# Reordering companion jobs, one output stage a pair earlier: a two-layer gated cross-attention kernel on one core

## The chip, the cores and the metric

One core of a Trainium2 chip runs the whole program in one launch. The metric is device time in microseconds, the median of several executions. Every time called "of the profile" comes from one further execution that was recorded instruction by instruction.

## The reference, cut to what matters

```
x = x + tanh(g_xattn[0]) * attn0(layernorm(x), ctx, ctx, mask)   # 16 heads of 32, no output projection
x = x + tanh(g_ffn[0])   * ffn0(layernorm(x))                    # 512 -> 2048 -> 2048 -> 2048 -> 512, SwiGLU, exact GELU
x = x + tanh(g_xattn[1]) * (attn1(layernorm(x), ctx, ctx) @ Wo.T + bo)
x = x + tanh(g_ffn[1])   * ffn1(layernorm(x))                    # 8-bit activations, ternary weights
```

`x` is 8 batches of 100 tokens of 512 numbers, `ctx` is 8 batches of 722 keys of 512. Queries, keys and values are float32, and the products of attentions and of the first feed-forward stage are made from a high and a low part of each operand (three products for each in the attentions), which is why most work comes in two halves: ScalarE (ACT) writes the high part, VectorE (DVE) or GpSimd (POOL) the low part.

## The kernel before, in words

The program has four stages in order of time: attention 0 (about 0 to 500 us), feed-forward 0 (500 to 1013 us), attention 1 (to about 1500 us) and feed-forward 1 (to the end). `L` is 0 or 1 for the attention.

An attention runs over `NP` = 64 pairs of heads, 8 pairs for each batch; `i` is the pair, `p` is `i % 8`. Each engine has its instructions in an order written out by hand, and engines wait for each other by semaphores alone. In pair `i` TensorE (PE) makes `scores(i + 1)`, `turn(i)` (the transposes of the exponentials), the companions of the pair, and `weigh(i - 1)` (the product with the values). DVE makes two `peak`s (the maxima of the scores of pair i + 1), `low_weighed(i - 2)` (takes the result of `weigh` out of PSUM), `low_turned(i)`, and the low part of each companion. ACT makes `high_weighed(i - 2)`, `high_turned(i)`, two `weights` (the exponentials of pair i + 1) and the high part of each companion. `scores(i + 1)` waits for the exponentials of pair i, since it overwrites their bank.

Companions are the projections of later batches, spread over the pairs by the table `BESIDE`: `("v", db, kt)` is a tile of 128 keys of V, `("k", db, g, half)` is half of the keys for K group `g` (four heads). The last, short tile of V of a batch is the tail job (`tail_job`, `high_tail`, `low_tail`, at the pairs of `tail_at`), packed with rows of the next batch. K halves are written to a staging tile `kst` (one for all groups, high and low), stored to HBM by `store_k`, and loaded in another layout by `load_k` into `KS`. `high_job` of a K half waits until the store of the group before has left its half of `kst`. The DMA orders are all given by SyncE (SP), in the order of its own loop.

The results of companions, of `weigh`, and of `project`, `turn_sums`, `turn_out` and `turn_normal` all go to two PSUM banks in turn. The list `RINGS` gives the turn order, and `ring_free(item)` makes PE wait until the item two places before has been taken out of its bank. For an item `("pv", i)` that is DVE's `low_weighed(i)`, for `("out", n)` DVE's `add_projected(n)`, and for `("xn", b)` ACT's `keep_normal`.

In attention 0 the finished batch b goes through `turn_out`, `add_out`, `stats_out`, `batch_root` (POOL), `normal_out` and `turn_normal` while later batches are worked on. In its last eight pairs `weigh` is made of 18 small products (`summed`), and there are no companions besides the one of pair 56.

At the end of attention 1 the 800 rows are cut into 7 output tiles. For tile n ACT and POOL write a high and a low part of the attention's result (`high_out`, `low_out`), PE multiplies by Wo (`project`, 12 products), SP has loaded the residual rows (`load_rows`), POOL has added the bias to them (`add_bo`), and DVE adds the product (`add_projected`) and takes mean and variance (`stats_projected`). POOL makes inverse roots (`tile_roots`), and `normal`, `scale_rows` and `quantize` lead to `turn_rows`, with which feed-forward 1 (`gate_and_up` first) begins. `OUT_AT` says in which pair each tile is projected.

## Time and profile before

| | us |
|---|---|
| median of 3 runs | 1588.3 |
| lowest and highest of them | 1586.6, 1588.71 |
| the profiled execution, whole | 1586.92 |
| its span (first to last instruction) | 1584.5 |
| PE busy in the span | 1565.0 |
| DVE busy | 1026.0 |
| ACT busy | 971.0 |
| POOL busy | 423.9 |

2.4 us of the profiled execution lie outside its span. Busy time of PE is a modelled figure: one matmul's end overlaps the next one's start, so a gap is a little longer than the idle time shown in brackets.

### The profile page before, as it was taken

To read this page: it belongs to the slowest core of one execution; us is meant where nothing else is said; L and a number is where in the kernel's file an instruction comes from. 1 tells how busy PE (TensorE), PEld (TensorE's weight loads), DVE (VectorE), ACT (ScalarE), POOL (GpSimd) and SP (SyncE) were. 2 spreads that over 40 slices of the span, in tenths; PEclk is the share of its full clock that TensorE was granted. 3 is DMA by queue.
4 is the path that set the end of the run, shared out by engine and by line. 5 is a ranking of instruction groups with operands and counts; after the bars stand their busy time and mean duration, and the time that the engine had idled before them with its cause. 6 is when DMAs were issued, how large, how long until landed. Compare 5 with 4: busy or idle time off the path is not lost.

```text
span 1584.5 us, 25762 instructions
## 1 busy us (share of the span) xinstructions
PE 1565.0 (99%) x9322; PEld 1427.5 (90%) x9322; DVE 1026.0 (65%) x1815; ACT 971.0 (61%) x2014; POOL 423.9 (27%) x569
## 2 busy tenths in 40 slices
PE   9999999999999999999999999999999999999999
PEld 7899899889888999999999998889999989988765
DVE  6577887787785563223544325647777777778987
ACT  5576777677665455444544435446677767666676
POOL 4121221222134222222222222311211121123751
PEclk9999999999999999999999999999999999999999
DMA  7766767677582325554365652576676677667500
GB/s 244 189 169 168 196 176 195 162 203 182 137 218 83 99 89 188 176 195 161 99 228 195 222 162 90 176 187 172 161 195 174 167 189 179 172 147 209 197 13 30
DMA packets 149974, 261.28 MB, mean 165 GB/s; under 512 B 41137, under 2 KB 94001, under 8 KB 149710
## 3 DMA queue, kind: packets, MB, share of 16 engines
q1 hardware_dynamic: 149505, 259.24, 58.3%
q8 instruction: 85, 1.39, 0.4%
q14 instruction: 52, 0.42, 0.1%
q10 hardware_dynamic: 332, 0.23, 0.0%
HBM read 191.01 MB, written 58.57 MB: 158 GB/s over the span
## 4 chain that ended last, share of the span: by engine, by line
PE 87%; DVE 6%; ACT 3%; DMA 2%; issue 1%; POOL 1%; SPq 0%; DVEq 0%; ACTq 0%
PE ps L1218 33%; PE ps L852 14%; PE ps L856 13%; PE ps L952 7%; PE ps L930 6%; PE ps L1152 2%; PE ps L1018 2%; PE ps L914 2%; PE ps L919 1%; DVE nmax L1367 1%; PE ps L1169 1%; PE ps L872 1%; ACT P L1909 1%; DVE PT L1373 1%; DMA kd<-ksl 1%
## 5 line engine op out<-in xcount | busy, mean ns | idle before, releaser
L1218 PE MATMUL ps<-ah_f,wh_f 128*128 128x400 f32 (+1 forms) x1296 | 442.9, 343 | 0.0
L1218 PE MATMUL ps<-al_f,wh_f 128*128 128x400 f32 (+1 forms) x1296 | 442.2, 342 | 0.0
L2272 POOL TENSOR_TENSOR cxl<-raw,cxh 128x384 fp32r<-128x384 f32 (+1 forms) x112 | 105.7, 965 | 562.7 <-ACT cxh L1851 562.7
L1773 DVE TENSOR_TENSOR wl_f<-raw_f,wh_f 128x1024 fp32r<-128x1024 f32 x85 | 103.7, 1223 | 231.9 <-POOL wh_f L2262 231.8
L1218 PEld LDWEIGHTS ps<-al_f,wh_f 128*128 128x128 f32 x1296 | 243.8, 188 | 0.0
L1218 PEld LDWEIGHTS ps<-ah_f,wh_f 128*128 128x128 f32 x1296 | 243.5, 188 | 0.1
L1367 DVE TENSOR_REDUCE nmax<-ps 100x1 f32<-100x722 f32 x256 | 220.6, 902 | 35.0 <-PE ps L918 31.4
L1909 ACT ACTIVATE P<-ps,nmax 100x722 f32<-100x722 f32 x256 | 219.9, 862 | 30.1 <-DVE nmax L1367 30.1
L1921 ACT ACTIVATE PT<-ps 128x400 fp32r<-128x400 f32 x384 | 165.9, 505 | 70.4 <-PE ps L930 69.2
L2190 ACT ACTIVATE raw_f<-wl_f 128x1024 f32<-128x1024 f32 x88 | 93.4, 1061 | 173.6 <-DVE wl_f L1773 173.0
L1373 DVE TENSOR_TENSOR PT<-ps,PT 128x400 fp32r<-128x400 f32 x384 | 196.3, 566 | 4.3 <-ACT PT L1921 1.1
L2262 POOL CAST wh_f<-raw_f 128x1024 fp32r<-128x1024 f32 x85 | 92.4, 1087 | 335.1 <-PE ps L1218 326.0
L852 PE MATMUL ps<-cxh,wkh 128*128 128x338 f32 (+1 forms) x512 | 173.3, 339 | 0.9 <-DVE cxl L1337 0.6
L852 PE MATMUL ps<-cxh,wkl 128*128 128x338 f32 (+1 forms) x512 | 167.8, 328 | 0.0
L852 PE MATMUL ps<-cxl,wkh 128*128 128x338 f32 (+1 forms) x512 | 167.0, 326 | 0.0
L952 PE MATMUL ps<-PT,V 128*128 128x400 f32 x720 | 152.2, 346 | 2.9 <-DVE V L1359 1.7
L930 PE MATMUL ps<-ident,P 100*128 100x100 f32 (+1 forms) x1536 | 153.1, 249 | 1.2 <-DVE PT L1373 1.2
L930 PEld LDWEIGHTS ps<-ident,P 100*128 100x128 f32 (+1 forms) x1536 | 143.1, 137 | 12.0 <-ACT P L1909 1.5
L952 PEld LDWEIGHTS ps<-PT,V 128*128 128x128 f32 x720 | 129.3, 188 | 10.2 <-DVE V L1359 6.5
L856 PE MATMUL ps<-wvh,cxh 128*128 128x512 f32 x320 | 131.5, 411 | 0.8 <-DVE V L1347 0.8
L1347 DVE SCALAR_TENSOR_TENSOR ksl<-ps,cols,ksh 128x384 fp32r<-128x384 f32 (+1 forms) x120 | 70.8, 590 | 94.9 <-ACT ksh L1862 94.9
L856 PE MATMUL ps<-wvh,cxl 128*128 128x512 f32 x320 | 126.1, 394 | 0.0
(226 smaller groups left out, 2665.2 us busy)
## 6 DMA issues: line engine op xcount, KB each, us to landing
KS<-kd SPq DMA_DIRECT2D x192, 361.0 KB
raw_f<-in_h SPq DMA_DIRECT2D x64, 512.0 KB, 3.9
raw_f<-in_gud SPq DMA_DIRECT2D x48, 512.0 KB, 4.3
raw<-in_ctx SPq DMA_DIRECT2D x64, 192.0 KB, 3.6
raw_f<-in_w SPq DMA_DIRECT2D x24, 512.0 KB, 3.9
kd<-ksh SPq DMA_DIRECT2D x60, 192.0 KB, 2.2
kd<-ksl SPq DMA_DIRECT2D x60, 192.0 KB, 2.5
raw<-in_ctx SPq DMA_DIRECT2D x64, 169.0 KB, 4.5
```

Of the source, the lines that this page charges most:

```text
L852: ins = e.matmul(o, m.wk[x][:, k, 128 * j[2]:128 * j[2] + 128], m.cx[y][:, k, off:off + n], start=(k == 0 and c == 0), stop=(k == 3 and c ...
L856: ins = e.matmul(o, m.cx[y][:, k, 128 * kt:128 * kt + KM[kt]], m.wv[x][:, k, :], start=(k == 0 and c == 0), stop=(k == 3 and c == 2))
L930: ins = e.transpose(ps[0:KM[kt], bank, o:o + S], m.P[0:S, (2 * i + h) % 3, 128 * kt:128 * kt + KM[kt]], ident[0:S, 0:S])
L952: ins = e.matmul(o, m.V[b % 2][0:r, kt, g, 128 * pr:128 * pr + 128], m.PT[0:r, i % 2, :, kt, :], start=(kt == 0), stop=(kt == KT - 1))
L1218: return e.matmul(o, p, q, start=start, stop=stop)
L1367: e.tensor_reduce(m.nmax[0:S, c:c + 1], scores_of(n), AX.X, ALU.max, negate=True).then_inc(v_max, 1)
L1373: e.tensor_tensor(lo, ps[:, bank, 0:400].rearrange("p (k n) -> p k n", k=2), raw32(hi), ALU.subtract).then_inc(v_t, 1)
L1773: e.tensor_tensor(wl[:, z, :], raw[:, r, :], raw32(wh[:, z, :]), ALU.subtract).then_inc(v_ul, 1)
L1909: e.activation(m.P[0:S, n % 3, :], scores_of(n), ACT.Exp, bias=m.nmax[0:S, c:c + 1], accum_out=m.rs[0:S, r:r + 1]).then_inc(a_exp, 1)
L1921: e.activation(m.PT[:, i % 2, 0, 2 * x:2 * x + 2, :], ps[:, bank, 0:400].rearrange("p (k n) -> p k n", k=2), ACT.Copy).then_inc(a_t, 1)
L2190: e.activation(raw[:, r, :], raw32(wl[:, z, :]), ACT.Abs, accum_out=low[:, z, 0:1]).then_inc(a_raw, 1)
L2272: e.tensor_tensor(m.cx[1][:, k, off:off + n], m.raw[:, k, off:off + n], raw32(m.cx[0][:, k, off:off + n]), ALU.subtract).then_inc(g_cx, 1)
```

## The change

1. `BESIDE`: in pair `p` = 4 K group 2's first half comes ahead of group 0's second half.
2. `tail_at`: the tail job of batch 0 goes from pair 1 to the end of pair 0, on PE, ACT and DVE. In the other pairs with a tail ACT takes it out between the two exponentials and not behind both.
3. Attention 0: the normalized rows of batch 5 (`normal_out`, `turn_normal`, `keep_normal`) go from pairs 56 and 57 to pairs 57 and 58, and DVE does `low_weighed(55)` ahead of both peaks of pair 57 instead of between them.
4. Attention 1: tile n is projected in pair 57 + n, not 58 + n. Its residual rows, bias, addition, statistics, roots, scaling and quantizing go with it by a pair each (the statistics of tiles 4 and 5 stand at pairs 61 and 63), and in pair 56 the first two tiles' rows are loaded ahead of that pair's `store_k`. `turn_rows(0)` stands behind `weigh(62)` and not ahead of it.

The amount of work is the same. The core of the diff (helpers of one line and the repetition of 2 in the ring lists are left out):

```
-          (("k", 1, 0, 1), ("k", 1, 2, 0)),
+          (("k", 1, 2, 0), ("k", 1, 0, 1)),
...
-    return i // 8 if i < NP and i % 8 == 1 and i // 8 % 4 < 3 else None
+    return i // 8 if i < NP and (i == 0 or i > 8 and i % 8 == 1) and i // 8 % 4 < 3 else None
...
+    if i == NP - 6:
+        return KEPT - 1
-    return i // 8 - 2 if i % 8 == 1 and 16 < i < NP else None
+    return i // 8 - 2 if i % 8 == 1 and 16 < i < NP - 8 else None
...
-OUT_AT = {58 + i: i for i in range(TILES - 1)}
+OUT_AT = {57 + i: i for i in range(TILES - 1)}
-STATS_AFTER = (59, 60, 61)
+STATS_AFTER = (58, 59, 60)
-OUT_FIRST = (60, 62)
+OUT_FIRST = (59, 61)
...
# SyncE
+                    if L and i == 56:
+                        w.wait_ge(p_pv, NP + 56)
+                        for n in range(2):
+                            load_rows(n)
                     for j in beside(i):
                         if j[0] == "k":
                             store_k(L, m, *j[1:])
...
                     if L and i == 57:
-                        w.wait_ge(p_pv, NP + 56)
-                        for n in range(4):
+                        for n in range(2, 4):
                             load_rows(n)
...
# TensorE
-                    if tail_at(i) is not None:
+                    if i and tail_at(i) is not None:
                         tail_job(tail_at(i))
                     for j in beside(i):
                         job(j)
+                    if i == 0:
+                        tail_job(0)
                     if L and i in OUT_AT:
                         project(OUT_AT[i])
+                    if i:
+                        weigh(i - 1)
                     if L and i == NP - 1:
                         turn_rows(0)
-                    if i:
-                        weigh(i - 1)
...
# VectorE
-                    early = scaled_at(i) is not None or L == 0 and i < NP - 7 and (
-                        out_at(i) is not None or turned_at(i) is not None)
-                    between = L == 0 and i == NP - 7
+                    early = scaled_at(i) is not None or L == 0 and (i == NP - 7 or i < NP - 7 and (
+                        out_at(i) is not None or turned_at(i) is not None))
...
+                    if L and i == 58:
+                        add_projected(0)
...
                     if i < NP:
                         low_turned(i)
-                    if L and i == 61:
+                    if L and i == 58:
+                        stats_projected(0)
+                    if L and i == 60:
                         scale_rows(0)
                     if L and i == 63:
                         inverse(B - 1)
                         scale_rows(1)
+                        stats_projected(5)
...
-                    if L == 0 and i == NP - 8:
+                    if L == 0 and i == NP - 7:
                         normal_out(i // 8 - 2)
...
+                    if i == 0:
+                        low_tail(0)
...
-                    if L and i in OUT_AT:
+                    if L and i in OUT_AT and i > 57:
                         add_projected(OUT_AT[i])
-                    if L and i in OUT_AT and i not in STATS_AFTER:
-                        stats_projected(OUT_AT[i])
+                    if L and i == 61:
+                        stats_projected(4)
...
# ScalarE
                     if i + 1 < NP:
                         weights(2 * i + 2)
+                    if i and tail_at(i) is not None:
+                        high_tail(tail_at(i))
                     if len(beside(i)) < 2 and i + 1 < NP:
                         weights(2 * i + 3)
-                    if L == 0 and i == NP - 7:
+                    if L == 0 and i == NP - 6:
                         keep_normal(turned_at(i))
...
                     for j in beside(i)[1:]:
                         high_job(j)
+                    if i == 0:
+                        high_tail(0)
...
# GpSimd
+                    if L and i == 58:
+                        tile_roots(0)
                     if L and i == 59:
-                        tile_roots(0)
-                    if L and i == 60:
                         normal(0)
-                    if L and i == 62:
+                    if L and i == 61:
                         quantize(0)
                     if L and i + 1 in OUT_AT:
                         low_out(OUT_AT[i + 1])
-                    if L and i == 60:
+                    if L and i == 59:
                         tile_roots(1)
                     if L and i == 57:
                         add_bo(0)
-                    if L and (57 <= i < 61 or i == 62):
-                        add_bo(min(i - 56, 5))
-                    if L and i == 63:
+                        add_bo(1)
+                    if L and 58 <= i < 62:
+                        add_bo(i - 56)
+                    if L and i == 62:
                         tile_roots(2)
```

## Rows read from the trace of the kernel before

**Rows 1.** The page, part 1: busy time and share of each engine.

```profile
PE 1565.0 (99%) x9322; PEld 1427.5 (90%) x9322; DVE 1026.0 (65%) x1815; ACT 971.0 (61%) x2014; POOL 423.9 (27%) x569
```

**Rows 2.** Windows: length, then busy us of PE, PEld, DVE, ACT, POOL.

```profile
1457.00:1500.00 43.00, 41.27 (x238) 32.83 (x237) 40.58 (x95) 28.42 (x66) 32.65 (x51) 1.00 0.74 238
```

**Rows 3.** Waits of PE over the span: us in total, times, longest.

```profile
PE ps L914 <- ACT P L1909: 2.2, 4, 0.7
PE ps L917 <- ACT P L1909: 2.0, 6, 0.4
PE ps L952 <- DVE V L1359: 1.7, 6, 0.4
...
PE ps L952 <- DVE ksl L1347: 1.2, 2, 0.7
...
PE ps L945 <- DVE QT L1392: 1.2, 1, 1.2
```

**Rows 4.** Timeline of ACT, pairs 0 and 1 of attention 0: start, us.

```profile
63.66 1.77 ACT L1851 ACTIVATE cxh<-raw 128x384 fp32r<-128x384 f32 x4
...
68.13 1.21 ACT L1890 ACTIVATE V<-ps 82x512 fp32r<-82x512 f32 x2
```

**Rows 5.** Timeline of DVE, pairs 0 to 2 of attention 0.

```profile
64.29 1.72 DVE L1367 TENSOR_REDUCE nmax<-ps 100x1 f32<-100x722 f32 x2
...
69.38 1.40 DVE L1359 TENSOR_TENSOR V<-ps,V 82x512 fp32r<-82x512 f32 x2 [1.93 <-ACT V L1890]
...
72.65 1.72 DVE L1367 TENSOR_REDUCE nmax<-ps 100x1 f32<-100x722 f32 x2 [0.64 <-PE ps L918]
```

**Rows 6.** Timeline of PE, first matmul of two scores, attention 0.

```profile
62.64 0.44 PE L914 MATMUL ps<-KS,QS 98*100 98x512 f32 x1 [0.53 <-ACT P L1909]
...
72.03 0.39 PE L914 MATMUL ps<-KS,QS 98*100 98x512 f32 x1
```

**Rows 7.** Timeline of ACT, the tail of pair 17, attention 0.

```profile
180.46 1.20 ACT L1890 ACTIVATE V<-ps 18x512 fp32r<-18x512 f32 x2
```

**Rows 8.** The chain that ended last: start, us, what.

```profile
207.70 4.19 DMA kd<-ksl
...
1466.62 2.97 PE ps L1067 x12
```

**Rows 9.** Timeline of DVE, pair 57, attention 0.

```profile
459.96 0.54 DVE L1392 TENSOR_TENSOR QT<-ps,sum 32x100 f32<-32x100 f32 x2
```

**Rows 10.** Timeline of PE, pairs 57 and 58, attention 0.

```profile
460.56 1.88 PE L945 MATMUL ps<-PT,V 128*64 128x200 f32 x18 [1.17 <-DVE QT L1392]
...
463.32 0.34 PE L917 MATMUL ps<-KS,QS 98*100 98x210 f32 x1 [0.36 <-ACT P L1909]
```

**Rows 11.** The line of `normal_out`: ns minimum, median, maximum.

```profile
L1490 DVE TENSOR_SCALAR x<-x,mv,rq x8: 536/537/1134, 175.3 to 498.8; 100x512 f32<-100x512 f32 x8
```

**Rows 12.** Timeline of DVE, end of attention 1.

```profile
1459.53 1.71 DVE L1367 TENSOR_REDUCE nmax<-ps 100x1 f32<-100x722 f32 x2
...
1462.13 1.53 DVE L1373 TENSOR_TENSOR PT<-ps,PT 128x400 fp32r<-128x400 f32 x3
1464.29 0.75 DVE L1423 SCALAR_TENSOR_TENSOR xr<-ps,gt,xr 115x512 f32<-115x512 f32 x1 [0.62 <-POOL xr L2315]
```

**Rows 13.** Timeline of PE, `weigh(56)` and `scores(60)`, attention 1.

```profile
1456.35 1.34 PE L952 MATMUL ps<-PT,V 128*128 128x400 f32 x6
...
1464.60 0.40 PE L914 MATMUL ps<-KS,QS 96*100 96x512 f32 x1
```

**Rows 14.** Timeline of POOL, end of attention 1.

```profile
1459.45 1.08 POOL L2308 TENSOR_TENSOR otl<-QT,oth 128x460 fp32r<-128x460 f32 x1 [4.71 <-ACT oth L1952]
1462.89 2.54 POOL L2315 TENSOR_TENSOR xr<-xr,bo 115x512 f32<-115x512 f32 x2 [2.35 <-DMA xr<-xs]
...
1468.35 0.23 POOL L2321 TENSOR_SCALAR rq<-mv 115x1 f32<-115x1 f32 x1
...
1471.23 0.19 POOL L2335 TENSOR_TENSOR rq<-rq 115x1 f32<-115x1 f32 x1
```

More of the change, by code:

```diff
@@ L160 @@
     for _l in range(2):
-        if tail_at(_i) is not None:
+        if _i and tail_at(_i) is not None:
             JOBS[_l].append(("v", tail_at(_i), KT - 1))
         JOBS[_l] += beside(_i)
+        if _i == 0:
+            JOBS[_l].append(("v", 0, KT - 1))
         if scaled_at(_i) is not None:
@@ L169 @@
             RINGS[_l].append(("xn", turned_at(_i)))
-        if tail_at(_i) is not None:
+        if _i and tail_at(_i) is not None:
             RINGS[_l].append(("v", tail_at(_i), KT - 1))
         RINGS[_l] += beside(_i)
+        if _i == 0:
+            RINGS[_l].append(("v", 0, KT - 1))
         if _l and _i in OUT_AT:
@@ L1625, in attention @@
                         peak(2 * i + 2)
-                        if between:
-                            low_weighed(i - 2)
                         peak(2 * i + 3)
-                    if i >= 2 and not early and not between and (L == 0 or i < NP):
+                    if i >= 2 and not early and (L == 0 or i < NP):
                         low_weighed(i - 2)
@@ L1643, in attention @@
                         scale_rows(1)
+                        stats_projected(5)
                     if L == 0 and i == NP - 1:
                         low_normal(KEPT)
-                    if L == 0 and i == NP - 8:
+                    if L == 0 and i == NP - 7:
                         normal_out(i // 8 - 2)
-                    if tail_at(i) is not None:
+                    if i and tail_at(i) is not None:
                         low_tail(tail_at(i))
@@ L2059, in attention @@
                     b, p = divmod(i, 8)
+                    if i >= 2:
+                        high_weighed(i - 2)
                     if L and i == NP:
                         turn_rows(0)
-                    if i >= 2:
-                        high_weighed(i - 2)
                     if i < NP:
@@ L2071, in attention @@
                         weights(2 * i + 2)
+                    if i and tail_at(i) is not None:
+                        high_tail(tail_at(i))
                     if len(beside(i)) < 2 and i + 1 < NP:
                         weights(2 * i + 3)
-                    if L == 0 and i == NP - 7:
+                    if L == 0 and i == NP - 6:
                         keep_normal(turned_at(i))
@@ L2077, in attention @@
                         high_normal(KEPT)
-                    if tail_at(i) is not None:
-                        high_tail(tail_at(i))
                     for j in beside(i)[:1]:
```

## Prediction

> **What bounds the kernel.** I read the page's busy shares first: PE is busy for 1565.0 of 1584.5 us [rows 1]. Nothing here takes work from PE, so the change can win only from PE's idle time, 19.5 us as modelled, and lose by adding to it. The waits of PE say where that idle time is and who ends it [rows 3]. Three kinds concern the change: `scores` waits for the exponentials (L914 and L917), `weigh` waits for the low part of a V tail (DVE L1359), and `weigh` waits for the low part of a K half (DVE L1347). A fourth is one wait for `low_weighed` (L1392) at the end of attention 0. The timelines give the places. The windows view shows the end of attention 1 to be different: in the 43 us from 1457 DVE is busy 40.58 and PE 41.27 [rows 2], so there DVE has no slack either, and PE can gain there only what DVE's own few gaps give.
>
> PE's idle time is taken from a matmul's modelled end, which lies about 0.15 us behind the next one's start; each wait below is worth that much more than its row shows.
>
> **Tail of batch 0 into pair 0, both attentions.** Now `scores(2)` waits 0.53 us and then 0.3 us more for exponentials [rows 6, 3], and `weigh(0)` a little for the tail's low part: about 1.5 us with the overlap. The K half of pair 0 ends at 61.95; with the tail's 12 matmuls (2.8 us) behind it `scores(2)` comes at 64.75 instead of 62.64 and waits for nothing. But the wait is not all gone. ACT does the four context copies of 63.66 (1.77 us) first, so its tail (1.21 us) runs from 65.3 to 66.5 [rows 4], and DVE's `low_tail` (1.40) from 66.5 to 67.9, now ahead of the peaks that ran at 64.29 [rows 5]. Those (1.72) end at 69.6, the two exponentials they free at 70.4 and 71.3. PE has by then done turn, V tile and `weigh(0)` (to 70.3) and finds the exponentials missing: `scores(3)` starts at 70.5 and ends near 71.9, where it now starts at 72.03 and ends at 72.7 [rows 6]. Gain 0.8 us, and the same in attention 1, where the same pairs show the same order and waits: 1.6 us. Bounds: 0 and 3.0.
>
> **ACT's tail between the exponentials.** Six waits of `weigh` for L1359 add up to 1.7 us, 0.4 the longest [rows 3]; two belong to the pairs above, four to pairs 17, 33, 41 and 49 of attention 0, where `keep_normal` makes ACT late. In pair 17 ACT begins the tail at 180.46, right behind the second exponential, though PE had finished it at about 179.9 (its first matmul at 176.9, plus 3.0) [rows 7]. Put ahead of it, it starts 0.5 us sooner, DVE follows, and the wait, 0.4 to 0.55 with the overlap, goes: 4 x 0.43 = 1.7 us. The second exponential ends 1.5 us later, 2 us before `scores` wants it, and in the pairs without `keep_normal` (ACT idle there until the tail is ready) 2.6 us later, also in time. Bounds: 0 and 1.9.
>
> **K groups in pair 4.** Group 2's store takes 4.19 us to land in the example of the chain, beside the loads of `KS` that SP orders right behind it [rows 8], and group 3's high part in pair 5 waits for it. Twice PE ends up waiting, 1.2 us in all [rows 3], 1.5 with the overlap. In the new order group 2's store goes out about 2 us earlier and with no load beside it, since `load_k` now waits for group 0's landing. The load comes some 2 us later, three pairs before its use; the stores of pair 5 queue behind it on SP and are wanted only in pair 7. Gain 1.4 us; bounds 0 and 1.5.
>
> **Batch 5's normalized rows.** `weigh(56)` waits 1.17 us for `low_weighed(55)` (459.96, 0.54 us) [rows 9, 10], because `normal_out` (1.13 us, begun at 457.1 [rows 11]) and a peak lie ahead of it on DVE. Without them `low_weighed(55)` ends at 458.6, both peaks at 460.3 instead of 461.4, the exponentials 1.2 us sooner. PE then meets a new wait of about 0.6: `weigh(57)`'s bank was `pv 56`'s, which DVE empties only after its peaks; but `scores(60)` loses its present waits of that kind. The next pair hangs on ACT, which waits for a weight tile that SP fetches behind the K store of pair 56; that store, waiting for DVE too, is 1.1 us sooner. Gain 1.2 us; bounds 0 and 2.
>
> **The end of attention 1.** PE: `project` (2.97 us, [rows 8]) goes in front of `weigh(56)`, now at 1456.35 [rows 13]. It needs `low_out(0)`, which POOL can begin after its last low part of Wo, at about 1455.5, for 1.08 us [rows 14]. So `project(0)` runs 1456.65 to 1459.5 and `scores(59)` starts at 1460.6. DVE starts the peaks of pair 58 at 1459.53 now, with no idle time [rows 12]; a peak starts 0.6 us behind its scores [rows 5, 6], so now it idles until 1461.2: 1.7 us. Then peaks 1.7, `low_weighed` 0.95, `add_projected(0)` 0.75: done at 1464.6. The residual rows (now in use at 1462.89 [rows 14]) come about a microsecond sooner and with the bias are ready at 1463.2, so they aren't late. But `project(1)` needs the bank of `out 0`, and PE was done with `turn(58)` at 1462.3: PE idles 2.3 us, and `project(1)` runs 1464.6 to 1467.5. DVE has by 1466.9 done `low_turned` (1.5) and the statistics (0.9), waits 0.7 for `project(1)`, then 0.7 for `scores(60)`, which starts at 1468.6, behind `weigh(57)`. Now it starts at 1464.60 [rows 13] with one project less done, 1467.4 by that count, so PE is 1.2 us behind. In pair 59 `low_out(2)` stands on POOL behind `tile_roots(0)`, 3.0 us from 1468.35 to 1471.4 now [rows 14], beginning after the statistics at 1467.0; `project(2)` waits 0.9 and DVE in turn 0.7. From `scores(61)` on DVE is full to the first gate product. Its idle time is 1.7 + 0.7 + 0.7 + 0.7 = 3.8 us against 0.8 now (0.62 at 1464.29 [rows 12] and 0.2 later; the rest of its 2.4 us of idle time in the window are gaps of some hundredths between instructions, which stay), so it comes 3.0 us later to the first gate product. The pair 63 that lost its project gives PE nothing, as PE waits for DVE there; `turn_rows(0)` behind `weigh(62)` costs nothing for the same reason, but would cost 0.9 if DVE were not late. I take +3.0; bounds -0.8 (DVE never idles) and +9 (below).
>
> One rule can be weighed here. That `normal_out` took 1.134 us, with POOL's split of batch 0 beside it, against a median of 0.537 over eight [rows 11]. The Trainium skill, SBUF: State Buffer, "Who interferes with whom", says that VectorE and GpSimd share a port pair as an exclusive lock, so that one waits out the other's instruction; the trace agrees with it by that row. By the rule `scale_rows(1)`, whose first instruction now would start together with POOL's `spread_sums`, pays about 0.6 us: the total below would be -2.3 instead of -2.9. The sum keeps to the row's median.
>
> **Sum.** -1.6 - 1.7 - 1.4 - 1.2 = -5.9 us; +3.0; together -2.9. The profiled execution took 1586.92 us, so 1584.0; it lies 1.4 below the median of 1588.3, so as a median 1585.4.
>
> **Rivals.** (a) Attention 1's end costs nothing: PE and DVE shift work without idling, as they do now from pair to pair. Against it speaks that `project(1)` needs an addition which needs peaks of scores made after `project(0)`. It gives -5.9 + (-0.8 to +0.7): 1581.6 to 1583.1. (b) The earlier gains are mostly not there: what I remove may be replaced by the next wait in line, as half of pair 0's is and a part of batch 5's; if that happens to the tails and the K groups too, each keeps half or less. With -2.5 for them all and +3.0: 1588.8. (c) Slower: every one of `project(1)` to `project(5)` waits as `project(1)` does, 2.3 us each, for the addition of the tile before: 11.5 us less the 0.8 of now and the 5.9 gained is +4.8, 1593.1. It decides once the five cost more than 9.1 together. Against it: from pair 60 on DVE is late with everything, and PE needs to wait for the peaks or for the addition, not both.
>
> **Chances.** My forecast 0.50, (a) 0.28, (b) 0.14, (c) 0.08. 0.2% is 3.2 us, about what a measurement of this kernel can tell from no change. The forecast's own range is 1583.5 to 1587 and straddles that line (1585.1), so half of it counts as faster: 0.24 + 0.27 = 0.51; same 0.26 + 0.01 + 0.13 = 0.40; slower 0.09. The range reaches from the best of (a), less a little for the runs' spread, to (b): 1580.8 to 1589.0.
>
> **What would show it.** Right: tail waits (L1359) down from six to none or two; no ACT wait for `kd` in pair 5 of batches 2 and 6; `scores(3)` waiting for exponentials; in attention 1 a DVE gap of 1.7 us ahead of the peaks of pair 58 and a PE gap above 2 us ahead of `project(1)`. Wrong: if that PE gap is missing, (a) holds; if it returns in pairs 59 to 62, (c). Late residual rows (`add_bo` starting after 1463) would add to it.

## The result, and the profile after

Before 1588.24 us, after 1601.25 us (medians of six runs each, lowest and highest after 1600.24 and 1603.41): ratio 1.0088, 95% interval 1.0078 to 1.0099, so the change costs 14.0 us. Forecast were 1585.4, and 1580.8 to 1589.0 as the range. The profiled execution took 1600.81 us, its span 1598.4, 13.9 more than before. Below, "+7.1 us" with a ratio is always the ratio less 1, times 1588, and what stands in brackets behind a ratio is its 95% interval; the interval of one kernel is 1.4 to 2.2 us wide to either side. One execution of the kernel without the K order took 5681 us beside eleven of 1588.4 to 1592.9, for a reason the record doesn't show, and is left out of its ratio.

Page, part 1, of the kernel after, the answer to [rows 1]:

```profile
PE 1568.3 (98%) x9322; PEld 1430.9 (90%) x9322; DVE 1027.2 (64%) x1815; ACT 973.1 (61%) x2014; POOL 423.5 (26%) x569
```

PE's work is the same, yet it is busy 3.3 us longer and idle 10.6 us longer: the first is a sign that some matmuls ran slower. The waits of PE over the span (us in total, times, longest), the answer to [rows 3]:

```profile
PE ps L961 <- DVE ksl L1358: 6.4, 7, 1.7
PE ps L1076 <- POOL otl L2325: 3.6, 3, 2.5
PE ps L923 <- ACT P L1924: 3.2, 4, 1.9
PE ps L1076 <- DVE xr L1434: 2.7, 2, 2.2
...
PE ps L1088 <- DVE PT L1384: 1.4, 1, 1.4
```

L961 is `weigh`, L1076 `project`, L923 `scores`, L1088 `turn_rows`. No wait for the tail's low part is among PE's waits any more (it had six). In its place `weigh` waits for the low part of a K half seven times and 6.4 us, where it had two and 1.2. `project` waits for `low_out` 3.6 us in all, where it had 0.2, and for `add_projected` 2.7, where it had 0.6. The wait of `turn_rows` for DVE is new.

Since PE has the same instructions in nearly the same order, the start of each `scores(k)`, after against before, tells where the time went:

| stretch | forecast | profile after |
|---|---|---|
| pairs 0 and 1, both attentions | -1.6 | -0.6 - 0.6 |
| tails of pairs 17, 33, 41, 49 | -1.7 | -1.5 |
| pair 5, two batches | -1.4 | -0.7 - 1.0 |
| pair 4, nine batches (0.2 to 1.9 each) | 0 | +8.1 |
| end of attention 0, from `scores(59)` | -1.2 | -1.05 + 2.8 |
| end of attention 1, from `scores(59)` | +3.0 | +9.1 |
| the rest, in steps of some hundredths | 0 | -0.6 |

**Pair 4.** SP, ACT and PE in pairs 3 and 4 of batch 1, attention 1, in the timeline of after (start, us, what; SP's rows are the issue of transfers, in brackets the idle time before and who ended it):

```profile
1143.08 2.53 SPq L772 DMA_DIRECT2D QS<-qh  x4
1145.65 1.25 SPq L772 DMA_DIRECT2D QS<-ql  x2
1146.94 2.53 SPq L772 DMA_DIRECT2D QS<-qh  x4
1149.52 1.24 SPq L772 DMA_DIRECT2D QS<-ql  x2
1150.86 0.53 SPq L738 DMA_DIRECT2D kd<-ksh  x1
1151.43 0.43 SPq L738 DMA_DIRECT2D kd<-ksl  x1
```

```profile
1155.63 0.58 ACT L1877 ACTIVATE ksh<-ps,cols 128x384 fp32r<-128x384 f32 x1 [2.37 <-DMA kd<-ksl]
```

```profile
1156.91 1.36 PE L961 MATMUL ps<-PT,V 128*128 128x400 f32 x6 [1.72 <-DVE ksl L1358]
```

Read upward: `weigh` waits for the low part of group 2's half, this for the high part, and this for the landing of the store of group 1's same half, which has to leave `kst` first. DVE finished that half at 1149.35 (L1358, 1148.73 for 0.62), but SP was giving out the twelve transfers of `spread_q` until 1150.8.

Why this wait is new, the same place in the kernel before shows (ACT, then PE):

```profile
1153.05 0.58 ACT L1862 ACTIVATE ksh<-ps,cols 128x384 fp32r<-128x384 f32 x1 [1.04 <-DMA kd<-ksl]
```

```profile
1152.61 1.26 PE L952 MATMUL ps<-PT,V 128*128 128x400 f32 x6
...
1155.35 0.42 PE L852 MATMUL ps<-cxh,wkh 128*128 128x384 f32 x1
```

There group 2's half waits for the same landing, and DVE is done with it at 1154.28 (L1347, 1153.66 for 0.62). But two PSUM banks are used in turn, and each item waits for the item two places before it. In the old order that is group 0's half for `weigh`, and nobody needs the bank of group 2's half before the first job of pair 5, at 1155.35: 1.1 us to spare. In the new order group 2's half stands two places ahead of `weigh`, which wants to start at the equivalent of 1152.61: 1.7 us too early, and the row of after says 1.72. What hid the landing was the 2.7 us of `weigh`, `scores` and `turn` between the two.

**End of attention 0.** The gain of batch 5's rows is there at `scores(59)` (-1.05). PE, then ACT, a few pairs later:

```profile
471.96 0.47 PE L923 MATMUL ps<-KS,QS 98*100 98x512 f32 x1 [1.89 <-ACT P L1924]
...
473.08 0.56 PE L928 MATMUL ps<-KS,QS 98*100 98x512 f32 x1
473.45 2.20 PE L939 MATMUL ps<-ident,P 100*128 100x100 f32 x12
```

`scores(61)` waits 1.89 us for exponentials that stand on ACT behind `measure_low(0)` (468.33, after 1.62 us of idle time ended by POOL's split of a weight tile, which had waited for its transfer). The fetch of that tile was given out 1.0 us sooner (458.62 against 459.66), and POOL could begin with it 0.5 us later (464.79 against 464.30). After the wait the same twelve transposes take 2.20 us instead of 1.19: the granted clock fell to its lower level.

**End of attention 1.** PE, DVE and POOL, and the window from 1450 to 1520 (its columns as in [rows 2]):

```profile
1463.89 0.75 PE L1076 MATMUL ps<-woh,oth 128*115 128x512 f32 x1 [2.49 <-POOL otl L2325]
1464.43 0.63 PE L1076 MATMUL ps<-wol,oth 128*115 128x512 f32 x1
...
1474.60 0.48 PE L1076 MATMUL ps<-woh,oth 128*115 128x512 f32 x1 [2.19 <-DVE xr L1434]
```

```profile
1471.19 1.73 DVE L1378 TENSOR_REDUCE nmax<-ps 100x1 f32<-100x722 f32 x2 [6.75 <-PE ps L927]
```

```profile
1453.83 1.58 POOL L2502 TENSOR_SCALAR bo<-bo,gt 128x512 f32<-128x512 f32 x1 [25.23 <-DMA bo<-in_bo]
1455.37 2.29 POOL L2317 CAST woh<-wos 128x512 fp32r<-128x512 f32 x4
1457.74 5.01 POOL L2320 TENSOR_TENSOR wol<-wos,woh 128x512 fp32r<-128x512 f32 x4
1462.71 1.08 POOL L2325 TENSOR_TENSOR otl<-QT,oth 128x460 fp32r<-128x460 f32 x1
```

```profile
1450.00:1520.00 70.00, 61.55 (x350) 49.53 (x348) 56.09 (x128) 40.28 (x93) 42.33 (x61) 0.95 0.59 180
```

The 2.19 us ahead of `project(1)` are what the prediction gave (2.3). DVE's gap ahead of the peaks of pair 58 is 6.75 us instead of the 1.7 of the forecast, since `scores(59)` stands behind `project(0)`, which is late and slow. The 2.49 ahead of `project(0)` aren't in the prediction: POOL began with the bias, and so with Wo behind it, 8.7 us later than in the kernel before (1445.10 there), while PE was only 4.8 late: the bias had landed late. SP gave out the loads of Wo and the bias 5.6 and 6.1 us later. And `project(0)`'s products, 0.40 us long at the full clock, take 0.63 (start to start 0.43 instead of 0.23): from 1463.89 to `weigh`'s start at 1469.12 it needs 5.2 us instead of 2.9.

### The profile page after: what moved, and what is told of

The parts are those of the page before. It is cut to its first block, busy times and chain, and to the rows that moved or that the text cites. A ratio compares the mean times of both kernels' runs of the same rounds, so it can differ in the third digit from the quotient of the medians.

```text
span 1598.4 us, 25762 instructions
## 1 busy us (share of the span) xinstructions
PE 1568.3 (98%) x9322; PEld 1430.9 (90%) x9322; DVE 1027.2 (64%) x1815; ACT 973.1 (61%) x2014; POOL 423.5 (26%) x569
## 4 chain that ended last, share of the span: by engine, by line
PE 80%; SPq 5%; DVE 4%; DMA 3%; ACT 3%; POOL 3%; issue 2%; DVEq 0%; ACTq 0%; POOLq 0%
PE ps L1229 32%; PE ps L865 12%; PE ps L861 10%; PE ps L961 6%; PE ps L939 6%; SPq L772 4%; PE ps L1163 2%; PE ps L1027 2%; PE ps L881 2%; DMA kd<-ksl 1%; PE ps L928 1%; PE ps L923 1%; PE ps L1180 1%; ACT P L1924 1%; DVE nmax L1378 1%
## 5 line engine op out<-in xcount | busy, mean ns | idle before, releaser
L961 PE MATMUL ps<-PT,V 128*128 128x400 f32 x720 | 153.3, 348 | 6.6 <-DVE ksl L1358 6.4
L961 PEld LDWEIGHTS ps<-PT,V 128*128 128x128 f32 x720 | 129.3, 188 | 15.5 <-DVE ksl L1358 9.1
L1358 DVE SCALAR_TENSOR_TENSOR ksl<-ps,cols,ksh 128x384 fp32r<-128x384 f32 (+1 forms) x120 | 71.0, 591 | 96.5 <-ACT ksh L1877 96.4
```

The costliest lines, as they stand in the source:

```text
L961: ins = e.matmul(o, m.V[b % 2][0:r, kt, g, 128 * pr:128 * pr + 128], m.PT[0:r, i % 2, :, kt, :], start=(kt == 0), stop=(kt == KT - 1))
```

## The experiments

Each of the four parts was first run alone in the kernel before. The parts are the pieces of the diff named 1 to 4 in the change, and together they are the kernel after.

### The K order alone

Part 1: the one line of `BESIDE`.

> The kernel before with one edit: in pair 4 of every batch group 2's half stands ahead of group 0's second half. Theory A (read from the trace after): the half placed first has its high part behind the landing of the store of pair 3, which SP issues only behind spread_q's twelve transfers; pair 4 then waits as it does in the kernel after, +6.4 us over both attentions net of the 1.7 us gained in pair 5, and Wo's and the bias's loads come some 4 us later, which costs nothing here because no tile needs them before pair 58: +6 to +7.5 us, ratio 1.004 to 1.0047. Theory B (the prediction): -1.4 us, ratio 0.9991; the new waits of pair 4 would then have come from the other parts of the change (the tail in pair 0, the ACT order) and be missing here.

Ratio 1.0045 (1.0031 to 1.0059), +7.1 us. By the starts of `scores` the new waits fall into pair 4 of nine batches, 0.25 to 1.73 us each (`weigh` waits for the low part of a K half eight times, 5.6 us), and pair 5 gains 0.7 and 1.0 in two. Theory A stands: the line costs this alone, with the old tails and ACT order.

### The output tiles alone

Part 4.

> The kernel before with the output tiles one pair sooner and two residual rows in pair 56, nothing else. Theory A: the kernel after lost some 9 us from scores(58) on, of which about 3 are the steps of the prediction and the rest comes from the late Wo and bias (an effect of the K order through SP's queue) and from the halved clock behind the 2.5 us wait it causes; with the old K order Wo and the bias are loaded near 1438, project(0) hardly waits for low_out(0), the granted clock stays at 1.00, and the whole costs +2 to +4 us, ratio 1.0013 to 1.0025. Theory B: the loss is the earlier tiles' own (POOL and DVE are late whatever the K order): +7 to +10 us, ratio 1.0044 to 1.0063, with the wait ahead of project(0) above 2 us and a clock below 1.00 in this stretch too.

Ratio 1.0036 (1.0022 to 1.005), +5.7 us: between the two. The wait ahead of `project(0)` is small (0.51), so its 2.5 us are indeed no property of the earlier tiles. But the clock falls here too, behind the wait for the addition. PE of this run:

```profile
1465.13 0.49 PE L1070 MATMUL ps<-woh,oth 128*115 128x512 f32 x1 [2.19 <-DVE xr L1426]
1465.46 0.39 PE L1070 MATMUL ps<-wol,oth 128*115 128x512 f32 x1
1465.69 0.49 PE L1070 MATMUL ps<-woh,otl 128*115 128x512 f32 x1
1465.98 0.63 PE L1070 MATMUL ps<-woh,oth 128*115 128x512 f32 x1
```

From its fourth product to its tenth `project(1)` runs at the lower level of the clock; from its start at 1465.13 to `weigh`'s at 1469.56 it takes 4.4 us instead of 2.9. DVE's next addition, which had been expected to wait 0.7, waits 2.42. The span is 7.0 longer than before.

### Batch 5's rows alone

Part 3.

> The kernel before with batch 5's normalized rows, and what is kept of them, one pair later in attention 0, nothing else. Theory A: pair 57 gains 1.1 us and pairs 60 to 62 lose 2.8 again, as in the kernel after, because measure_low(0) waits for POOL's prepare(0), whose fetch lands no sooner, and PE's wait there is followed by matmuls at the lower clock: +1.5 to +2 us, ratio 1.0010 to 1.0013. Theory B (the prediction): -1.2 us, ratio 0.9992; the loss behind it in the kernel after would be from the K order, whose late store stands in front of the fetch on SP.

Ratio 1.0003 (0.9994 to 1.0012), +0.5 us. Inside attention 0 the profile gives -1.06 at `scores(59)`, then +0.92 and +0.34: +0.2. The gain is given back with the old K order too, so B is out (its 0.9992 lies just below the interval). A's range (from 1.0010) begins inside the interval, so A isn't out, but in the profile the part costs less than A says: the slow matmuls of after's `scores(62)` (+1.62) are not part of it. PE waits 1.61 us ahead of `scores(61)` here, and the clock stays at 1.00 there. The span of this profile is 2.7 longer all the same: 2.2 arise at the end of attention 1, which the edit doesn't touch: ACT waited for the landing of pair 56's store (0.81 us), `scores(59)` for the exponentials behind it (1.17), and the clock was 0.91 from 1460 to 1480. The profile before has 0.42 for that wait and no fall, but those of other kernels with the old tiles have 0.83 (the K order alone), 1.08 (its store in the middle), 0.90 and 1.17 (the two mixtures), the last two with a fall of the clock, so up to 2.2 us of a difference between two profiles can come from this place alone. The eleven runs lie between 1587.5 and 1591.7.

### The tails alone

Part 2.

> The kernel before with batch 0's tail behind the K half in pair 0 and ACT's tail between the exponentials, nothing else. Both traces agree with the prediction here: 0.6 us twice in pairs 0 and 1 and four times 0.3 to 0.5 in the pairs behind 17, 33, 41 and 49: -2.7 us, ratio 0.9983. The rival: what is gained in the middle of attention 0 is given back at its end, where PE waits for a fetch that does not come sooner, and only the part of attention 1 stays: -0.6 us, ratio 0.9996.

Ratio 0.9979 (0.997 to 0.9988), -3.3 us; the profile -2.65, in steps of -0.6 twice and -0.3 to -0.5 four times. This is the prediction's step, as worked out.

The four alone add up to 7.1 + 5.7 + 0.5 - 3.3 = +10.0. The whole is +14.0. The intervals of the four and of the whole, combined, come to some 4 us, so the 4.0 between them are barely clear of noise by these runs.

### All but the K order

```
-          (("k", 1, 2, 0), ("k", 1, 0, 1)),
+          (("k", 1, 0, 1), ("k", 1, 2, 0)),
```

> The kernel after with the old K order in pair 4, all else as in the kernel after. The parts alone measured +7.1 us (K order), +5.7 (tiles), +0.5 (batch 5's rows) and -3.3 (tails), together +10.0, and the whole +14.0, so 4 us come from parts acting on each other. Theory A: these 4 us are the K order's hold on SP, which makes the bias and Wo late for the earlier tiles and the store of pair 56 late for attention 0's end; without the K order all of it goes: +3 us against before, ratio 1.0018 (sum of the three parts: -3.3 + 0.5 + 5.7 = +2.9). Theory B: the 4 us come from the tails or rows acting on the tiles; they stay: +7 us, ratio 1.0043.

Ratio 1.0019 (1.001 to 1.0028), +3.0 us, and the other three parts' sum is +2.9: no sign that they act on each other. B's 1.0043 lies outside the interval, theory A's 1.0018 in its middle. Inside the whole, then, the K line costs 14.0 - 3.0 = 11.0 us (give or take 2), of which 7.1 alone and about 4 (give or take 3) in what it does to the other parts. This run also shows the end of attention 1 without a late bias and, as it happened, without a fall of the clock. DVE's idle times there, and the window:

```profile
1458.72 1.73 DVE L1378 TENSOR_REDUCE nmax<-ps 100x1 f32<-100x722 f32 x2 [1.81 <-PE ps L927]
...
1465.18 0.75 DVE L1434 SCALAR_TENSOR_TENSOR xr<-ps,gt,xr 115x512 f32<-115x512 f32 x1 [0.84 <-PE ps L1076]
...
1466.70 1.73 DVE L1378 TENSOR_REDUCE nmax<-ps 100x1 f32<-100x722 f32 x2 [0.61 <-PE ps L927]
...
1473.19 0.36 DVE L1399 TENSOR_TENSOR sum<-ps,sum 64x200 f32<-64x200 f32 x1 [0.61 <-ACT sum L1951]
```

```profile
1450.00:1520.00 70.00, 63.03 (x361) 47.53 (x361) 62.45 (x143) 43.99 (x92) 46.57 (x62) 1.00 0.47 153
```

The forecast had 1.7 + 0.7 + 0.7 + 0.7 for these four, and they are 1.81, 0.84, 0.61 and 0.61. Two more follow that it didn't have, 0.64 (at 1492.95) and 0.56 (ahead of the first product by the gate). From `scores(58)` to the end this execution, the fastest of its eleven, loses 4.2 us instead of the 3.0 of the forecast.

### The store of pair 3 in the middle of `spread_q`

In the kernel before, with the K order of the change:

```
                 for r in range(3):
                     for j in range(2):
                         spread(r, j, ...)
+                if middle:
+                    middle()            # store_k of pair 3's K half
                 for r in range(3):
                     for j in range(2, 4):
                         spread(r, j, d_qs[z])
```

> The kernel before with the K order of the change, and in pair 3 SP issues the two store transfers of pair 3's K half after six of spread_q's twelve transfers instead of after all twelve. In the run with the K order alone the half was ready at 369.97, in SP's queue behind spread_q until 371.50, and weigh then waited 1.29 us near 375.5. Theory A (SP's queue is the cause): the store goes out 1.5 us sooner and most of the new waits of pair 4 go; left are the 1.7 us gained in pair 5 less at most 2 us of rest: -1.7 to +1 us against before, ratio 0.9989 to 1.0006. Theory B (the landing is slow, or pair 4 has too little work ahead of the second half, whoever is first in SP's queue): the waits stay and it costs +5 to +7 us, ratio 1.0031 to 1.0044.

SP of this run, the same place as above:

```profile
1143.56 1.24 SPq L763 DMA_DIRECT2D QS<-ql  x2
1147.28 0.33 SPq L729 DMA_DIRECT2D kd<-ksh  x1
1147.65 0.43 SPq L729 DMA_DIRECT2D kd<-ksl  x1
1148.13 3.41 SPq L763 DMA_DIRECT2D QS<-qh  x4
```

Ratio 0.9996 (0.9988 to 1.0005), -0.6 us: 7.7 less than with the store behind all twelve. `weigh` waits for no K half any more in this profile, and pair 5's gains (-0.7, -1.0) are kept. So the place of the store in SP's order is what the 7.7 us hang on: in the kernel after, the half stood ready for 1.5 us before its turn in that queue. Whether the K order with this store is any faster than the kernel before, these runs don't tell, since the interval holds 1.

### PE kept at work ahead of `project(1)`

In the kernel with the tiles alone, in pair 58 behind `scores(59)`; the result goes to a bank that `turn(58)` then overwrites:

```
+                    if L and i == 58:
+                        w.wait_ge(v_t, 3 * (NP * L + i - 1) + 1)
+                        for _ in range(7):
+                            e.matmul(ps[0:S, 3, :], wo[0][:, 0, 0:S], wo[0][:, 0, :], start=True, stop=True)
                     turn(i)
```

> The kernel with the output tiles alone one pair sooner, and in pair 58, between scores(59) and turn(58), seven extra matmuls of 512 columns on data that is already there, whose result is overwritten unread. They take 7 x 0.23 = 1.6 us of the 2.2 us that PE idles ahead of project(1). Theory A (the clock behind the idle time is 1.6 us of the cost): project(1) starts at the same time as without them but runs at the full clock, 2.97 us instead of 4.4, so scores(60) comes some 1.5 us sooner and the kernel takes 1 to 1.6 us less than with the tiles alone: +4 to +4.7 us against before, ratio 1.0026 to 1.003. Theory B (the clock does not follow PE's own idle time): project(1) is as slow as without them, and turn(58) 1.6 us later besides: +5.7 us or more.

```profile
1461.66 1.77 PE L1091 MATMUL ps<-woh 128*100 128x512 f32 x7
...
1465.04 0.48 PE L1070 MATMUL ps<-woh,oth 128*115 128x512 f32 x1 [0.58 <-DVE xr L1430]
1465.36 0.39 PE L1070 MATMUL ps<-wol,oth 128*115 128x512 f32 x1
```

`project(1)` starts at the same time (1465.04, 1465.13 without the seven) and takes 2.9 us instead of 4.4; the step at `scores(60)` is +1.5 instead of +3.1, the clock 1.00 in the whole window, the span 2.6 us shorter. Of the 1.6 us gained at `scores(60)`, 0.9 are given back at `scores(61)` (+0.6 with the seven, -0.3 without). The other 1.6 of the 2.6 arise behind `scores(63)`, where both kernels wait 1.4 us ahead of `turn_rows(0)` and the clock is 0.92 from 1500 to 1520 without the seven, 1.00 with them. In the runs the difference is small: 1.0032 (1.002 to 1.0044), +5.1 against +5.7, between the theories, and the profiled execution was the fastest of six. One profile each doesn't show that the seven products kept the clock up: without them, in the kernel without the K order, it didn't fall behind the same wait either.

The mean granted clock of every execution is on record, and it bounds what the clock costs: the time lost by it is at most the span times (1 - clock), and less where PE waits for others anyway. As estimates from these means: the kernel before loses 0.6 to 0.8 us in this way, the K order alone 0.3, the tiles alone 3.5 (0.9978 over five executions), the same with the seven products 1.6 (0.9990 over six), the kernel without the K order 3.0, the kernel after 5.9 (0.9963 over six, from 0.995 to 0.997). So at most about 3 of the tiles' 5.7 us and 5 of the whole 14.0 are the lower clock, and the 7.1 of the K order alone aren't.

### Wo and the bias loaded sooner, in the kernel after

```
+                    if L and i == 52:
+                        ...                      # the block of pair 53, with its waits
                     if p == 4 and b + 1 < B:
                         load_k(L, m, b + 1, 0)
...
-                    if L and i == 53:
-                        w.wait_ge(g_cx, 112)
-                        w.wait_ge(p_job, tail_done(L, B - 1))
-                        e.dma_start(wos[:, :, :], t["wo1"]).then_inc(d_out, 16)
-                        e.dma_start(bo[:, :], ...).then_inc(d_out, 16)
```

> The kernel after with the loads of Wo and the bias issued in pair 52 ahead of load_k instead of in pair 53. In the kernel after SP issued them at 1443.5, behind the KS load that had to wait for group 0's landing until 1439.85; here they go out near 1435. Theory A (their lateness is what the K order adds to the earlier tiles): project(0) no longer waits 2.5 us for low_out(0), the clock does not fall behind that wait, and the kernel takes 3 to 4.5 us less than the kernel after: +9.5 to +11 us against before, ratio 1.006 to 1.007. Theory B (POOL and DVE are late for other reasons): at most 1 us less, ratio 1.0082 or more.

Ratio 1.0074 (1.0062 to 1.0087), +11.8 us, 2.2 less than after, with intervals that overlap. This lies between the ranges of the two theories. In the profile the wait ahead of `project(0)` is gone as in A. But the load of 1 MB for Wo now goes out at 1436.07, ahead of the `KS` load at 1439.65, and this lands late:

```profile
1449.78 0.48 PE L923 MATMUL ps<-KS,QS 96*100 96x512 f32 x1 [2.34 <-DMA KS<-kd]
```

`scores(57)` waits 2.34 us for it, so this profile's span is the same 1598.4. The lateness is moved, not removed, and how much of the 4 us between the parts and the whole it is, this run doesn't show.

### `turn_rows(0)` back ahead of `weigh(62)`

The kernel with the tiles alone, with `turn_rows(0)` on PE and on ACT where it was.

> The kernel with the output tiles alone one pair sooner, with turn_rows(0) where it was before: on PE ahead of weigh(62), on ACT ahead of high_weighed(62). The prediction costed this move at nothing and said 0.9 us if DVE is not late. In the runs with the tiles sooner PE waits 1.4 us for PT ahead of turn_rows(0) and 0.65 us for xTq ahead of the first gate product, and DVE 0.55 us or more ahead of the first product by sg; before has none of these. Theory A: the move is worth about 1.2 us: both waits shrink, +4.5 us against before where the tiles alone measured +5.7, ratio 1.0028. Theory B: whoever stands first, PE waits there for the same DVE work (the last PT of pair 63), and nothing changes: +5.7, ratio 1.0036.

```profile
1498.79 0.36 PE L1082 MATMUL ps<-idb,xq 115*128 115x115 bf16 x4 [2.60 <-DVE PT L1376]
```

One wait of 2.60 us in place of 1.40 and 0.65 (and a fall of the clock from 1500 to 1520, 0.93, as there: 0.92). Ratio 1.005 (1.0036 to 1.0063), +7.9; the span is 1591.6, where it was 1591.5. A's gain isn't there. The profile is B's: both orders wait for the same DVE work. The runs are 2.2 us above the tiles alone, with intervals that overlap, so moving `turn_rows(0)` behind `weigh(62)` cost nothing, as the prediction had it, and may have gained a little.

### The kernel after with the store in the middle of `spread_q`

> The kernel after with one edit on SP: the store of pair 3's K half goes out after six of spread_q's twelve transfers. By the parts alone the K order then costs -0.6 instead of +7.1. Theory A (the 4 us of interaction also come from SP being late behind that store): everything hangs on those 1.5 us, Wo and the bias are loaded near 1437 again and what is left is tails -3.3, rows +0.5, tiles +5.7, K -0.6: +2.3 us against before, ratio 1.0014. Theory B (the interaction comes from load_k(7,0) in pair 52 waiting for the store of pair 4 whatever SP did in pair 3): the 4 us stay, +6.3 us, ratio 1.004.

Ratio 1.0026 (1.0015 to 1.0036), +4.1 us: 9.9 less than after by one edit of SP's order, and 1.1 more than without the K line at all, with intervals that overlap. So most of the K line's 11.0 us inside the whole hang on that store. The result lies midway between A (+2.3) and B (+6.3), both just outside its interval, and picks neither. The profiled execution was the slowest of eight (1594.89, the median 1591.77), and its clock fell four times. In it pair 4 costs nothing any more. What is left is 3.0 us at `scores(62)` of attention 0, behind a wait of 1.49 us and a fall of the clock, and the end of attention 1:

```profile
1456.59 0.74 PE L1078 MATMUL ps<-woh,oth 128*115 128x512 f32 x1 [2.04 <-POOL otl L2327]
```

`load_k` of pair 52 still waits for group 0's landing (given out at 1433.05, before at 1430.50, while PE is 2 us ahead of before), the bias (out at 1437.57) is in use at 1446.51, and `low_out(0)` comes late for `project(0)` again; the clock is 0.84 from 1450 to 1470. That the K line does this whatever SP does in pair 3 is read from this one profile, not tested.

### Two mixtures of what was worth keeping

The kernel before with parts 1 and 2 and the store in the middle of `spread_q`; and the same with part 3 and

```
-    MEASURED = (58, 61, 62)
+    MEASURED = (59, 61, 62)
```

> The kernel before with the tails of the change, its K order with the store in the middle of spread_q, batch 5's rows one pair later, and measure_low(0) in pair 59 instead of 58. Batch 5's rows alone gained 1.06 us at scores(59) and gave 1.26 back at scores(60) and (61), the last where ACT stands 1.35 us in measure_low(0) waiting for POOL's split of a weight tile that landed no sooner. Theory A: with measure_low(0) a pair later ACT is free, the give-back at scores(61) goes, and this kernel is 1 to 1.7 us faster than the same without rows and measure_low moved (the next run): ratio to before 0.9968. Theory B: the next thing in line (POOL's split, the transfer) holds pair 60 or 61 just as long: the same as the next run or slower by up to 1 us.

> The kernel before with the tails of the change and its K order with the store of pair 3 in the middle of spread_q. The two alone measured -3.3 and -0.6 us. Theory A: they touch different pairs and add up: -3.9 us, ratio 0.9975, faster than both kernels. Theory B: they meet on ACT and SP in pair 1 and pair 4 of each batch and the K part is lost again: -2 to -3.3 us, ratio 0.998 to 0.9988.

The one without part 3: ratio 0.998 (0.9971 to 0.9989), -3.2 us, no more than the tails alone (-3.3), so not the sum of theory A; its interval reaches both theories. In its profile the K part's -0.7 and -1.0 are there and so are the tails' steps, but `scores(62)` loses 1.59: behind a wait of 0.89 us at 469.32 the clock fell. The one with part 3: 0.9968 (0.9957 to 0.9979), -5.1 us, clear of both kernels and the lowest ratio here. ACT in it (L1918 is the exponentials, L2201 `measure_low`):

```profile
466.86 0.86 ACT L1918 ACTIVATE P<-ps,nmax 100x722 f32<-100x722 f32 x1
467.61 0.20 ACT L1918 ACTIVATION_READ_ACCUMULATOR P<-ps,nmax 100x1 f32 x1
467.70 1.06 ACT L2201 ACTIVATE raw_f<-wl_f 128x1024 f32<-128x1024 f32 x1
```

`measure_low(0)` starts without idle time, `scores(61)` gains 1.41 against before, and `scores(62)` gives 1.81 back. It isn't ACT that holds it, but the next thing in line, a load of `KS`:

```profile
473.23 0.47 PE L922 MATMUL ps<-KS,QS 98*100 98x512 f32 x1 [1.65 <-DMA KS<-kd]
```

So from `scores(58)` to `scores(63)` part 3 with this move gains nothing against before (-1.05 + 0.93 - 1.41 + 1.81 - 0.28 = 0). Against the other mixture the profile is 1.2 us shorter, which is no more than the other mixture loses at `scores(62)` to its fall of the clock. The ratio is 0.0012 lower (1.9 us), the median 0.9 us, with intervals that overlap: that part 3 is worth anything here isn't shown.

## Why the prediction was wrong, step by step

- **Tails.** Right in mechanism, places and nearly in size: -3.3 forecast, -2.65 in the profile and -3.3 in the runs of that part alone. The six waits for the tail's low part are gone, and `scores(3)` waits for exponentials (0.27 us), as the prediction's signs had it.
- **"K groups in pair 4 ... Gain 1.4 us; bounds 0 and 1.5."** This is the step that failed. Its gain came (-1.7 in the profile after), but it had costed at nothing the half that is now first: its high part needs the landing of the store of pair 3, this store stands on SP behind `spread_q`, and `weigh` now needs that half's bank. Before, `weigh` needed the other half's, and the step neither named that turn nor said what it costs when it changes. Measured +7.1 alone, +11.0 inside the whole, -0.6 with the store 1.5 us sooner. The forecast's total with this one term replaced by the 11.0 that it measured inside the whole would be -1.6 - 1.7 - 1.2 + 3.0 + 11.0 = +9.5; the two steps below make up the other 4.4 (1.7 and 2.7).
- **Batch 5's rows.** The 1.2 us at `weigh(56)` were right (-1.05), and so was the new wait of 0.6 for the bank (0.49). Wrong was that the next pair's fetch would follow the store of pair 56 and come sooner: given out 1.0 us sooner, it landed no sooner. Why is open: the loads of `KS` stand in front of it, and the transfers' mean busy share is 0.92 from 455 to 475, but no run moved them. +0.5 in the runs instead of -1.2.
- **The end of attention 1, +3.0.** The chain was right nearly gap by gap: 1.81, 0.84, 0.61, 0.61 of DVE against 1.7 and three times 0.7, and 2.19 ahead of `project(1)` against 2.3. Mis-sized by two later gaps of DVE (0.64 and 0.56): 4.2 in the execution at full clock, 5.7 (3.5 to 7.9) in the runs. Its missing terms are the clock, which fell behind the PE gap in some executions (1.6 us at `scores(60)`, 0.9 of them given back behind it), and in the whole the late bias, which the step took from before's rows though part 1 moved SP's loads.
- **The rule on the shared port.** The Trainium skill, SBUF — State Buffer, "Who interferes with whom", says that where VectorE and GpSimd contend, the one that issues first keeps the shared ports for its whole instruction and the other is blocked. The prediction took this for a price of 0.6 us on `scale_rows(1)` beside `spread_sums`. The rows, DVE and POOL of after:

```profile
1507.98 0.45 DVE L1455 TENSOR_SCALAR hs<-xr,mv,rq 115x512 f32<-115x512 f32 x1
```

```profile
1508.13 0.77 POOL L2311 COPY rx<-rr 100x512 f32<-100x512 f32 x1 [3.89 <-DVE rr L1412]
```

  DVE started first and took 0.45 us, less than the 0.54 to 0.60 of its five other instances; POOL's copy took 0.77 where its others take 0.60 to 0.62. So 0.16 fell on POOL and nothing on DVE. The trace agrees with the page on who pays, though the 0.16 are less than the 0.30 us by which the two overlap, and the sum was right to leave the 0.6 out.
- **The rivals.** None held. (c) had PE waiting for every addition; it waits 2.2 and 0.5 in two of five. The forecast's own sign that it was wrong, late residual rows, came true in the kernel after (in use at 1467.1, the bound was 1463), but cost nothing there: they were ready at 1469.6, and DVE came to the first addition at 1473.80.

What stays open: how much of the tiles' 5.7 us is the lower clock (at most about 3 by the granted clock of the executions), and of the 4 us between the sum of the parts and the whole, which share is the late bias and which the clock. By the same means the whole loses some 2 us more to the clock than the four parts together.

## What to carry to other kernels

When two jobs change places, cost each of them in its new place, not only the one that was meant: for the one that comes first, ask what its first instruction waits for, who issues that transfer, what stands ahead of it in that queue, and who will wait for its result. Where banks are used in turn, a new order gives the same job another one that waits; the work that used to stand between the two is cover, and it has a length. A part that makes one queue later must be carried into every other part that is costed from rows of before, loads without a near user too, since these reach their use only tens of microseconds on. And a wait on an engine that hardly ever waited may cost more than itself.

## What the runs showed of the hardware

TensorE's granted clock, 1.00 in the profile before from 440 to 520 and from 1440 to 1520, fell to its lower level (1.2 GHz) in most of the other profiles and stayed there for some 3 to 7 us; a product of 512 columns then starts every 0.43 us instead of 0.23. Ahead of each fall stands a wait of PE, but a longer wait doesn't make the fall certain. Falls came behind single waits of 2.60, 2.49, 2.19, 2.04, 1.89, 1.49, 1.40, 1.17, 0.90, 0.89 and 0.82 us, most of them with a shorter one (0.37 or 0.65) right behind. None came behind 1.17 and 1.25 in the profile before, nor behind 2.34 in the kernel with Wo loaded sooner. The same 2.19 us ahead of `project(1)` were followed by a fall in four profiles (the tiles alone, `turn_rows(0)` back, Wo sooner, after with the store in the middle) and by none in two (the kernel after and the kernel without the K line). PE in the last:

```profile
1462.13 0.49 PE L1076 MATMUL ps<-woh,oth 128*115 128x512 f32 x1 [2.19 <-DVE xr L1434]
1462.46 0.39 PE L1076 MATMUL ps<-wol,oth 128*115 128x512 f32 x1
...
1462.92 0.39 PE L1076 MATMUL ps<-woh,oth 128*115 128x512 f32 x1
```

The Trainium skill, TensorE: Matmul & The Clock Gate, "Part 1: The HAM clock gate", says of the start of a kernel that how many matmuls run at the lower clock differs between runs of one kernel. The runs here agree for its middle: the granted clock of the five executions of the tiles alone lies between 0.997 and 0.999, and the longer executions are those with the lower clock (1592.22 us at 0.999, 1595.61 at 0.997). Seven products of no use, put into the gap, went with a full clock at that place in one profile.
